# x added to the last stage's root rows on GpSimd, shares of two experts from five operations, first scatters without a bound

## The chip, the cores and the metric

The kernel runs on one core of a Trainium2 chip. The metric is the device time of one execution in microseconds; the times shown are medians of several executions. The engines that matter are TensorE (PE: matrix products and transposes), VectorE (DVE), ScalarE (ACT), GpSimd (POOL: here powers of small columns, and the starting of scatters by row index) and SyncE (SP, which starts most transfers). Times within the trace are microseconds from the start of the span.

## The reference, cut to what matters

```python
# x: 3125 x 256, 50000 edges (src, dst)
h   = relu(sage(layernorm(x), W1_l, W1_r, b1))
x   = x + sage(h, W2_l, W2_r, b2)          # sage: mean over neighbours @ W_l + own row @ W_r + b
t   = layernorm(x)
p   = softmax(t @ router_w.T);  rw, re = top_k(p, 2)
rw  = rw / max(rw.sum(-1), 1e-12)          # the shares of the two experts chosen
out = x + t + sum over e of combine[:, e] * (gelu(t @ w1[e] + b1[e]) @ w2[e] + b2[e])
```

## The kernel before

The 3125 nodes are 25 tiles of 128 rows (the last has 53). A dense adjacency matrix of 25 x 25 blocks stays in SBUF in 16 bits, so the mean over neighbours is 25 products of 128x512 a tile. The program has four stages: projection of the normalised x, aggregation of the first layer with projection for the second, aggregation of the second layer together with routing (the "last stage" of the graph part, tile by tile, from about 291 to 446 us), and rounds of the experts (from 470 us to the end). The change lies in the third of these; I call it stage 3.

In stage 3 each tile t goes through this loop. PE adds up 25 products (L1306) into one of four PSUM buffers; among the products of tile t+2 stands the transposition of the normalised rows of tile t (`turn_token`, L1380, ahead of the fourth product), then its router scores (L1391), and once in four tiles three small products of `prefix` (L1398 to L1401, ahead of the eighth product). SP loads two buffers for each tile: `zi`, the root rows (own row @ W2_r + b2) from DRAM, and `xt`, the rows of x. There is one of each, so SP waits for the semaphore `zx_taken` before it loads the next tile (`node_tile`, L456 and L457). On the same queue SP also stores the finished row sums of the tile, and in tiles 8 to 15 it starts three loads of expert weights a tile, after the store and ahead of the next tile's loads.

DVE's part of a tile is `x2_and_var` (L1008: zi + xt; L1012 and L1013: plus both halves of PE's sum, scaled; L1016 to L1019: mean and variance), then, after GpSimd's power (`root`, L581), `norm_and_sum` (L1026: normalised rows, which PE transposes; L1031: the row sum that SP stores). After tiles 4, 8, 12, 16, 20 and 23, and once more at the end, DVE runs `choose` for a batch of up to four tiles: it finds the two best experts, makes 0/1 masks for PE's `prefix` (up to L1063) and the two shares (L1066 to L1072). In tiles 6, 10, 14, 18, 22 and 24, and at the end, `place` turns PE's prefix sums into row numbers (`slots`, L1095). GpSimd, which executes in program order, starts two scatters a tile (L593; tile 0: L589, with a bound on the row numbers) as soon as the slots of the batch are there; a scatter of tile t-6 is queued behind the power of tile t. Ahead of the first power stand eight plain transfers (L605). At the end of the stage, scatters of tiles 17, 18 and 19 stand between the powers of tiles 23 and 24, and those of tiles 20 to 24 behind them.

DVE and GpSimd operate on `rows` (which holds xt and zi), `zt` (the row sum), `stat` and columns of `onehots`.

## Time and profile before

| | us |
|---|---|
| median of 3 runs | 595.81 |
| lowest, highest | 594.27, 596.04 |
| the profiled execution | 592.88 |
| its span | 591.2 |
| PE busy | 554.3 |
| DVE busy | 364.7 |
| GpSimd busy | 185.5 |
| mean granted clock of PE | 0.984 |

PE is busy in nearly all of the span. The exceptions are the first slice of 15 us and the passage from stage 3 to the experts, at 444 to 470 us. A row of the trace gives start, duration, engine, line, operation, tile written and tiles read, and in square brackets the idle time just before and what ended it.

### The profile page before, as it was taken

The numbers are of one execution on the slowest core, as the hardware profiler recorded it, in microseconds if no ns is written. First come the engines' busy times: TensorE is split into PE (matmuls) and PEld (weight loads), VectorE is DVE, ScalarE is ACT, GpSimd is POOL, SyncE is SP. The second block draws the span as 40 slices with busy tenths as digits, with TensorE's granted clock in tenths as the row PEclk, the third lists the DMA queues.
The fourth block names the chain that finished last, engine by engine and source line by source line (L and its number), as shares of the span: only waits on it lengthen the run. The fifth ranks groups of instructions, "written<-read, shape, count | busy, mean of one in ns | idle before, by whom it ended". The sixth has DMA issues, their size and how long they took to land.

```text
span 591.2 us, 11509 instructions
## 1 busy us (share of the span) xinstructions
PE 554.3 (94%) x3050; PEld 336.3 (57%) x3051; DVE 364.7 (62%) x1219; ACT 222.2 (38%) x422; POOL 185.5 (31%) x180
## 2 busy tenths in 40 slices
PE   4999999999999999999999999999991499999996
PEld 3555555555555555555445555555551488888885
DVE  5998667667657667663255766767678334444442
ACT  4676845434444434443101100000000155555554
POOL 3751000000000000000040154443356237787887
PEclk9999999999999999999999999999996799999999
DMA  8421211111111111012642146673332757787776
GB/s 259 148 79 60 65 45 54 48 34 54 44 37 55 37 44 54 28 55 53 196 129 80 55 137 200 202 245 126 106 130 97 228 109 118 125 142 129 129 116 92
DMA packets 64343, 61.24 MB, mean 104 GB/s; under 512 B 11281, under 2 KB 62334, under 8 KB 64302
## 3 DMA queue, kind: packets, MB, share of 16 engines
q1 hardware_dynamic: 47422, 44.84, 25.2%
q0 software_dynamic: 11200, 14.40, 13.1%
q10 hardware_dynamic: 5680, 1.49, 1.2%
q8 instruction: 21, 0.34, 0.2%
q14 instruction: 20, 0.16, 0.1%
HBM read 32.34 MB, written 29.30 MB: 104 GB/s over the span
## 4 chain that ended last, share of the span: by engine, by line
PE 69%; DMA 9%; DVE 8%; issue 8%; POOL 4%; SPq 1%; ACT 0%; POOLq 0%; DVEq 0%; ACTq 0%
PE bank L1306 22%; PE counts_ps L1448 8%; PE bank L1459 8%; PE bank L1221 8%; PE bank L1296 7%; PE counts_ps L662 7%; PE counts_ps L1306 4%; POOL xs_dram L593 2%; DMA rows<-in_x 2%; PE counts_ps L1439 2%; DMA xs_dram<-w,onehots 2%; DMA y<-y_dram 2%; PE bank L1211 1%; POOL stat L581 1%; PE bank L1289 1%
## 5 line engine op out<-in xcount | busy, mean ns | idle before, releaser
L1306 PE MATMUL bank<-y,adj 128*128 128x512 f16 x625 | 154.7, 379 | 0.4 <-ACT zt L1519 0.4
L1306 PE MATMUL counts_ps<-y,adj 128*128 128x512 f16 x625 | 144.0, 379 | 2.0 <-DMA y<-y_dram 2.0
L669 ACT ACTIVATE adj<-counts_ps 128x1000 f32 (+1 forms) x80 | 80.2, 1005 | 59.2 <-PE counts_ps L662 59.2
L635 POOL DMA_INDIRECT out<-adj x56 | 88.4, 1578 | 37.9 <-ACT adj L1654 18.5
L1306 PEld LDWEIGHTS counts_ps<-y,adj 128*128 128x128 f16 x625 | 60.7, 101 | 64.7 <-DMA y<-y_dram 4.3
L1306 PEld LDWEIGHTS bank<-y,adj 128*128 128x128 f16 x625 | 57.9, 97 | 59.5 <-issue 13.7
L565 POOL IOTA onehots<- 128x8 int32 x1 | 0.1, 143 | 225.4 <-PE counts_ps L662 225.4
L1448 PE MATMUL counts_ps<-adj 128*128 128x256 f32 x240 | 57.0, 380 | 0.0
L662 PEld LDWEIGHTS counts_ps<-onehots 125*128 125x128 f16 x640 | 42.4, 98 | 23.6 <-ACT adj L669 11.0
L648 DVE TENSOR_TENSOR onehots<-iota,lo_t 125x1024 f16<-125x1024 f16 x80 | 54.7, 684 | 1.8 <-issue 0.9
L1618 ACT ACTIVATE rows<-bank 128x256 f32<-128x256 f32 x25 | 9.6, 384 | 123.0 <-PE bank L1380 123.0
L648 DVE TENSOR_TENSOR onehots<-iota,key_t 125x1000 f16<-125x1000 f16 x80 | 53.7, 671 | 0.0
L1459 PE MATMUL bank<-adj 128*128 x224 | 53.0, 379 | 0.0
L662 PE MATMUL counts_ps<-onehots 125*128 125x125 f16 x640 | 51.0, 221 | 0.3 <-DVE onehots L648 0.3
L1221 PE MATMUL bank<-w,rows 128*128 128x512 f32 x100 | 48.8, 611 | 1.5 <-issue 1.3
L1448 PEld LDWEIGHTS counts_ps<-adj 128*128 128x128 f32 x240 | 44.9, 190 | 7.2 <-issue 1.2
L1296 PE MATMUL bank<-w,rows 128*128 128x512 f32 x100 | 47.0, 592 | 0.0
L1459 PEld LDWEIGHTS bank<-adj 128*128 128x128 f32 x224 | 40.5, 190 | 4.4
L1654 ACT ACTIVATE adj<-adj 128x256 f32<-128x256 f32 x56 | 25.4, 501 | 46.0 <-DVE adj L1175 46.0
L581 POOL TENSOR_TENSOR stat<-stat 128x1 f32<-128x1 f32 x25 | 14.2, 570 | 72.8 <-DVE stat L1019 72.8
L1175 DVE TENSOR_TENSOR adj<-bank,adj 128x512 f32<-128x512 f32 x28 | 19.4, 691 | 27.1 <-PE bank L1459 27.1
L1512 ACT ACTIVATE yo<-bank,scl_i 128x256 f16<-128x256 f32 x23 | 10.9, 475 | 58.1 <-PE bank L1296 58.1
(237 smaller groups left out, 646.6 us busy)
## 6 DMA issues: line engine op xcount, KB each, us to landing
adj<-xs_dram SPq DMA_DIRECT2D x31, 264.0 KB
rows<-z_dram SPq DMA_DIRECT2D x49, 128.0 KB, 2.1
z_dram<-zt SPq DMA_DIRECT2D x33, 128.0 KB, 1.7
adj<-in_L_ffn_w SPq DMA_DIRECT2D x16, 256.0 KB, 3.2
rows<-in_x SPq DMA_DIRECT2D x24, 128.0 KB
out<-yo SPq DMA_DIRECT2D x24, 128.0 KB
y_dram<-yo SPq DMA_DIRECT2D x23, 128.0 KB, 1.7
y<-y_dram SPq DMA_DIRECT2D x4, 640.0 KB, 6.8
```

The source lines that it names most:

```text
L581: g.tensor_tensor(stat[:, 8:9], stat[:, 9:10], stat[:, 10:11], ALU.pow).then_inc(S["rstd_in"], 1)
L635: g.indirect_dma_start(out, bass.IndirectOffsetOnAxis(ap=ids[u][:, h:h + 1], axis=0), ye[u][:, h, :], None, bounds_check=N - 1, oob_is_err ...
L648: last = nc.vector.tensor_tensor(oh[0:RUN, slot, :].rearrange("p (g k w) -> p g k w", k=n, w=HALF), iota_4[0:RUN, 0:n, :].rearrange("p (g ...
L662: last = nc.tensor.matmul(counts_ps[:, 2 * slot + bank_of, at * P:at * P + KEYS], stat_g[:, :, h:h + 1].rearrange("p k a -> p (k a)"), mov ...
L669: nc.scalar.activation(adj[:, :, bass.ds(at, GW * WD)].rearrange("p b (h d) -> p b h d", d=WD), counts_ps[:, 2 * (group % 2):2 * (group % ...
L1175: v.tensor_tensor(ysum[s], y_ps[s], ew(eb2_sb, e, 0).rearrange("p (h n) -> p h n", h=1) .to_broadcast((P, 2, D)), ALU.add).then_inc(S["ysu ...
L1221: last = te.matmul(out_of[t % 2][:, :], nrm_t_of[t % 2][:, k * P:(k + 1) * P], w[:, k, :], start=(k == 0), stop=(k == KD - 1))
L1296: last = te.matmul(bank[1][:, :], nrm_t[:, k * P:(k + 1) * P], w[:, k, :], start=(k == 0), stop=(k == KD - 1))
L1306: last = te.matmul(to, adj[:, b, t * P:(t + 1) * P], y[:, b, :], start=(b == 0), stop=(b == NT - 1))
L1448: last = te.matmul(hid_ps[s][:, m * PAIR:(m + 1) * PAIR], w1_of[s][:, k, m * P:(m + 1) * P], xe_t[s][:, k * PAIR:(k + 1) * PAIR], start=(k ...
L1459: last = te.matmul(y_ps[s][:, h, :], ge_t[s][:, m * PAIR + h * P:m * PAIR + (h + 1) * P], ew(ew2_sb, e, m), start=(m == 0), stop=(m == KD ...
L1654: a.activation(ye[u][:, h, :], ysum[s][:, h, :], ACT.Copy, scale=tab_c[:, bass.ds(i * 2 + h, 1)]).then_inc(S["ye_in"], 1)
```

## The change

Three things. First, the addition zi + xt leaves DVE (L1008 is gone). GpSimd does it in place into `xt` (`add_root`) and signals `x_added`. DVE's first operation of a tile now reads PE's sum and `xt`, and only this operation frees both buffers for the next loads. Second, the shares come from five operations in place of seven: both exponentials are summed on their own, this sum is bounded below by 1e-12 times the sum of all eight, and the exponentials are multiplied by its reciprocal. Third, the two scatters of tile 0 no longer have a bound.

```diff
+            def add_root(t):
+                pool.wait_ge(S["z_in"], 16 * (t + 1 + NT))
+                pool.wait_ge(S["x_in"], 16 * (t + 1))
+                g.tensor_tensor(xt[:, :], xt[:, :], zi[:, :], ALU.add).then_inc(S["x_added"], 1)
+
             def scatter(t, j):
...
                 for k in range(TOPK):
-                    if t == 0:
-                        g.indirect_dma_start(xs_dram, bass.IndirectOffsetOnAxis(
-                            ap=slots[:, t * TOPK + k:t * TOPK + k + 1], axis=0), tok[t % KEPT], None,
-                            bounds_check=NE * REGION - 1, oob_is_err=False).then_inc(scattered[t % 2], 16)
-                    else:
...
             pool.sem_inc(S["tok_free"], KEPT)
+            add_root(0)
...
                 root(t)
+                if t + 1 < NT:
+                    add_root(t + 1)
                 if BATCH + 2 <= t < NT - 1:
                     scatter(*to_scatter[t - BATCH - 2])
...
-                dve.wait_ge(S["z_in"], 16 * (t + 1 + NT))
-                dve.wait_ge(S["x_in"], 16 * (t + 1))
-
+                dve.wait_ge(S["x_added"], t + 1)
...
-                v.tensor_tensor(zt[:, :], zi[:, :], xt[:, :], ALU.add).then_inc(S["zx_taken"], 1)
-                dve.wait_ge(S["zx_taken"], t + 1)
                 dve.wait_ge(S["agg"], t + 1 + NT)
                 d = rdeg[:, bass.ds(t, 1)]
-                link(v.scalar_tensor_tensor(zt[:, :], counts_ps[:, s, 0:D], d, zt[:, :], ALU.mult, ALU.add))
+                v.scalar_tensor_tensor(zt[:, :], counts_ps[:, s, 0:D], d, xt[:, :], ALU.mult, ALU.add
+                                       ).then_inc(S["zx_taken"], 1)
+                dve.wait_ge(S["zx_taken"], t + 1)
...
+                v.tensor_reduce(resum, ex[:, :, 0:TOPK], AX.X, ALU.add)
                 link(v.tensor_reduce(esum, ex, AX.X, ALU.add))
+                link(v.scalar_tensor_tensor(esum, esum, 1e-12, resum, ALU.mult, ALU.max))
                 link(v.reciprocal(resum, esum))
-                link(v.tensor_tensor(prob, ex[:, :, 0:TOPK], each(resum, TOPK), ALU.mult))
-                link(v.tensor_reduce(esum, prob, AX.X, ALU.add))
-                link(v.tensor_scalar(esum, esum, 1e-12, None, ALU.max))
-                link(v.reciprocal(resum, esum))
```

GpSimd's queue at the start of stage 3, before: the eight plain transfers, then seven powers (tiles 0 to 6) and the scatters of tile 0.

```order
L605 DMA xs_dram<-biases 32x264 [waits zeros]
L605 DMA xs_dram<-biases 32x264 x7
L581 TENSOR_TENSOR stat<-stat 128x1 [waits var_in] x7
L589 DMA xs_dram<-w,onehots 27648x264 [waits slots]
L589 DMA xs_dram<-w,onehots 27648x264
```

The same place now (the power is L580, the addition L585).

```order
L604 DMA xs_dram<-biases 32x264 [waits zeros]
L604 DMA xs_dram<-biases 32x264 x7
L585 TENSOR_TENSOR rows<-rows 128x256 [waits x_in,z_in]
L580 TENSOR_TENSOR stat<-stat 128x1 [waits var_in]
L585 TENSOR_TENSOR rows<-rows 128x256 [waits x_in,z_in]
```

The addition of tile 0 now stands behind the eight transfers, and each later one behind the power of the tile ahead of it, where it waits for two loads.

GpSimd's queue at the end of stage 3, before, from the scatters of tile 17 to the power of tile 24.

```order
L593 DMA xs_dram<-w,onehots 27648x264 [waits slots]
L593 DMA xs_dram<-w,onehots 27648x264
L593 DMA xs_dram<-w,onehots 27648x264 [waits scattered0,slots]
L593 DMA xs_dram<-w,onehots 27648x264
L593 DMA xs_dram<-lo_t,onehots 27648x264 [waits slots]
L593 DMA xs_dram<-lo_t,onehots 27648x264
L581 TENSOR_TENSOR stat<-stat 128x1 [waits var_in]
```

The same place now.

```order
L585 TENSOR_TENSOR rows<-rows 128x256 [waits x_in,z_in]
L592 DMA xs_dram<-w,onehots 27648x264 [waits slots]
L592 DMA xs_dram<-w,onehots 27648x264
L592 DMA xs_dram<-w,onehots 27648x264 [waits scattered0,slots]
L592 DMA xs_dram<-w,onehots 27648x264
L592 DMA xs_dram<-lo_t,onehots 27648x264 [waits slots]
L592 DMA xs_dram<-lo_t,onehots 27648x264
L580 TENSOR_TENSOR stat<-stat 128x1 [waits var_in]
```

The addition of tile 24 stands ahead of six scatters, and the power of tile 24 still behind them.

DVE's queue of one tile, before, and behind it the same piece now.

```order
L1008 TENSOR_TENSOR zt<-rows 128x256 [waits u_ready,x_in,z_in]
L1012 SCALAR_TENSOR_TENSOR zt<-counts_ps,rdeg,zt 128x256 [waits agg,zx_taken]
L1013 SCALAR_TENSOR_TENSOR zt<-counts_ps,rdeg,zt 128x256 [waits dve_chain]
L1016 BN_STATS stat<-zt 128x6 [waits sums_free]
L1018 BN_AGGR stat<-stat 128x2 [waits dve_chain]
L1019 TENSOR_SCALAR stat<-stat 128x1 [waits dve_chain]
```

```order
L1010 SCALAR_TENSOR_TENSOR zt<-counts_ps,rdeg,rows 128x256 [waits agg,u_ready,x_added]
L1013 SCALAR_TENSOR_TENSOR zt<-counts_ps,rdeg,zt 128x256 [waits zx_taken]
L1016 BN_STATS stat<-zt 128x6 [waits sums_free]
L1018 BN_AGGR stat<-stat 128x2 [waits dve_chain]
L1019 TENSOR_SCALAR stat<-stat 128x1 [waits dve_chain]
```

The operation that frees the load buffers now also waits for PE's sum of the tile (`agg`).

## Rows read from the trace of the kernel before

**Rows 1.** The page, busy time of each engine with its share.

```profile
PE 554.3 (94%) x3050; PEld 336.3 (57%) x3051; DVE 364.7 (62%) x1219; ACT 222.2 (38%) x422; POOL 185.5 (31%) x180
```

**Rows 2.** Busy time by stretch: stretch, length, PE, PEld, DVE, ACT, POOL, clock, DMA.

```profile
355.00:380.00 25.00, 25.00 (x139) 13.43 (x136) 17.22 (x75) 1.77 (x5) 10.44 (x12) 1.00 0.70 219
```

**Rows 3.** Timeline, start of stage 3: start, duration, engine, operation, count, [idle before].

```profile
300.07 4.16 POOL L605 DMA_DIRECT2D xs_dram<-biases  x8 [0.49 <-DVE biases L986]
...
304.25 0.61 POOL L581 TENSOR_TENSOR stat<-stat 128x1 f32<-128x1 f32 x1
304.97 0.41 DVE L1026 TENSOR_SCALAR w<-zt,stat 128x256 f32<-128x256 f32 x1 [1.73 <-POOL stat L581]
...
305.91 0.38 PE L1380 MATMUL bank<-ident,w 128*128 128x128 f32 x2
...
311.88 0.38 PE L1380 MATMUL bank<-ident,w 128*128 128x128 f32 x2
```

**Rows 4.** Groups by form, engine POOL: busy us, mean ns of one, idle before.

```profile
L527 POOL IOTA iota<- 128x256 f16 x1 | 1.5, 1517 | 0.0
...
L530 POOL TENSOR_SCALAR_AFFINE_SELECT ident<-ident 128x128 f32<-128x128 f32 x1 | 0.3, 283 | 0.0
...
L567 POOL TENSOR_SCALAR_AFFINE_SELECT onehots<-onehots 128x1 f32<-128x1 f32 x1 | 0.2, 187 | 26.4 <-DVE onehots L983 26.4
```

**Rows 5.** Timeline of tiles 5 and 6, where DVE is catching up.

```profile
331.55 0.42 DVE L1008 TENSOR_TENSOR zt<-rows 128x256 f32<-128x256 f32 x1
332.01 0.48 DVE L1012 SCALAR_TENSOR_TENSOR zt<-counts_ps,rdeg,zt 128x256 f32<-128x256 f32 x1
332.16 0.33 SPq L456 DMA_DIRECT2D rows<-z_dram  x1
...
334.09 0.55 POOL L581 TENSOR_TENSOR stat<-stat 128x1 f32<-128x1 f32 x1 [8.01 <-DVE stat L1019]
...
335.99 0.42 DVE L1008 TENSOR_TENSOR zt<-rows 128x256 f32<-128x256 f32 x1 [0.37 <-DMA rows<-in_x]
```

**Rows 6.** Timeline, DVE's L1008 of tiles 9, 12, 13 and 17.

```profile
355.28 0.42 DVE L1008 TENSOR_TENSOR zt<-rows 128x256 f32<-128x256 f32 x1
...
371.37 0.42 DVE L1008 TENSOR_TENSOR zt<-rows 128x256 f32<-128x256 f32 x1 [1.32 <-DMA rows<-in_x]
...
379.67 0.42 DVE L1008 TENSOR_TENSOR zt<-rows 128x256 f32<-128x256 f32 x1
...
403.37 0.42 DVE L1008 TENSOR_TENSOR zt<-rows 128x256 f32<-128x256 f32 x1
```

**Rows 7.** Timeline: the masks of the batch of tiles 8 to 11 and PE's prefix.

```profile
378.25 0.16 DVE L1063 TENSOR_TENSOR onehots<-onehots 128x16 f16<-128x16 f16 x1
...
378.83 0.18 PE L1398 MATMUL bank<-onehots 128*128 128x32 f16 x1
```

**Rows 8.** Timeline: shares and slots of the last batch.

```profile
454.76 0.18 DVE L1066 TENSOR_REDUCE onehots<-onehots 128x4 f32<-128x32 f32 x1
...
456.08 0.17 DVE L1072 TENSOR_TENSOR key_t<-onehots 128x8 f32<-128x8 f32 x1
...
457.63 0.17 DVE L1095 CAST onehots<-onehots 128x8 uint32<-128x8 f32 x1
```

**Rows 9.** Timeline of POOL from the power of tile 23 to the last scatter.

```profile
439.43 0.57 POOL L581 TENSOR_TENSOR stat<-stat 128x1 f32<-128x1 f32 x1 [0.97 <-DVE stat L1019]
...
443.95 0.96 POOL L593 DMA_INDIRECT xs_dram<-w,onehots  x1 [1.46 <-DMA xs_dram<-w,onehots]
...
448.73 0.61 POOL L581 TENSOR_TENSOR stat<-stat 128x1 f32<-128x1 f32 x1
...
456.17 0.96 POOL L593 DMA_INDIRECT xs_dram<-onehots  x1 [0.30 <-issue]
458.62 0.96 POOL L593 DMA_INDIRECT xs_dram<-onehots  x1 [1.50 <-DVE onehots L1095]
...
462.42 0.96 POOL L593 DMA_INDIRECT xs_dram<-w,onehots  x1 [0.31 <-issue]
```

More of the change, by code:

```diff
@@ L233, in build @@
         resum = later([BATCH], F32)
-        prob = later([BATCH, TOPK], F32)
         hist = later([NB + 1, NE], F32)
@@ L587, in scatter @@
                 for k in range(TOPK):
-                    if t == 0:
-                        g.indirect_dma_start(xs_dram, bass.IndirectOffsetOnAxis(
-                            ap=slots[:, t * TOPK + k:t * TOPK + k + 1], axis=0), tok[t % KEPT], None,
-                            bounds_check=NE * REGION - 1, oob_is_err=False).then_inc(scattered[t % 2], 16)
-                    else:
-                        g.indirect_dma_start(xs_dram, bass.IndirectOffsetOnAxis(
-                            ap=slots[:, t * TOPK + k:t * TOPK + k + 1], axis=0),
-                            tok[t % KEPT], None).then_inc(scattered[t % 2], 16)
+                    g.indirect_dma_start(xs_dram, bass.IndirectOffsetOnAxis(
+                        ap=slots[:, t * TOPK + k:t * TOPK + k + 1], axis=0),
+                        tok[t % KEPT], None).then_inc(scattered[t % 2], 16)
                 if 0 < t <= NT - KEPT:
```

5 lines of the change are left out of this document (3 added, 2 removed).

## Prediction

> **What bounds the kernel.** I read the page's busy times first, then busy time by stretch for stage 3, then the timeline at its start, in its laps and at its end. PE is busy for 94% of the span [rows 1], and inside stage 3 for 25.00 of 25 us at full clock, while DVE has 17.22 and GpSimd 10.44 of them [rows 2]. So within the stage DVE and GpSimd cost nothing as long as PE is never kept waiting, and every moment in which it is goes straight into the time. PE's beat is 311.88 - 305.91 = 5.97 us a tile [rows 3], and four tiles with one prefix take about 23.97 us (4 x 5.97 and some 0.07 for the prefix). Behind the stage, from 444 to 470 us, PE idles and a serial chain decides: power of tile 24, its normalised rows, scores, masks, slots, the last four scatters, their landing, the first loads of the experts. What GpSimd and DVE lose or gain there counts in full, too.
>
> **The new operation's price.** The trace has no addition of 128x256 on GpSimd. A select over one input of 128x128 took 283 ns and of 128x1 187 ns [rows 4]: 0.75 ns a column, so 256 columns from one input would be 0.38 us, and two inputs read one after the other 0.57 us. DVE needs 0.42 for the same addition [rows 5]. Upward the nearest row is an iota of 128x256 with 1.52 us [rows 4]. I take 0.7 us, near the doubled select; bounds 0.4 and 1.5.
>
> The Trainium skill (GPSIMD Engine Reference, section 3, Performance versus the Vector engine) has a two-input addition of 2048 fp32 columns at 4497 ns on GpSimd against 2293 ns on DVE, and its rule is to leave elementwise work to VectorE; scaled to 256 columns its slope alone would be an estimated 0.56 us, and the sum below would stay within 0.3 us of mine. No run here shows it yet.
>
> **Start of the stage: +2.4.** This term is the surest. GpSimd is busy with eight plain transfers until 304.23, and the power of tile 0 starts at 304.25 [rows 3]. The addition of tile 0 now stands behind the same transfers, where DVE before could add without GpSimd. Addition 304.25 to 304.95, 0.1 for the signal, DVE's first operation at 305.05. From this operation to the power it takes 334.09 - 332.01 = 2.08 us [rows 5], from the power to the normalising operation 304.97 - 304.25 = 0.72 [rows 3], so that one runs from 307.85 to 308.26. PE transposed that tile at 305.91, 0.53 after the rows were ready [rows 3]; now it can at 308.3. PE waits 2.4 us (2.1 with an addition of 0.4, 3.2 with 1.5). It has no other work ahead of this in its queue, and as it is then busy without a gap to the end of the stage, nothing gives this back.
>
> **The laps: +0.5.** Before, DVE's addition freed the buffers before PE's sum had to be there. Now the first operation that also needs PE's sum frees them, and the addition follows the landing. A lap in which DVE catches up is thus: operation 0.48, SP starts 0.19 after it (332.16 against 331.97), from SP's start to the landing 3.83 (335.99 - 332.16) [rows 5], addition 0.7, signal 0.1: 5.3 us, where it was 4.44 (335.99 - 331.55). It still beats PE's 5.97, so in most laps this is hidden behind PE's products. In the laps with choose DVE gets 0.46 shorter by the addition and about 0.55 by the shares (below), which pays back more than one such lap.
>
> The tight place is tiles 8 to 15, where three loads of weights stand ahead of the next tile's loads on SP's queue. Tile 9 to 13 took 379.67 - 355.28 = 24.39 us, tile 13 to 17 23.70 [rows 6], against 23.97 of PE; DVE stood waiting for the load, 1.32 us ahead of tile 12. After the change: the lap with choose -1.01; three laps bound by a transfer +0.86 each (0.7 + 0.1 + 0.06, since 0.48 stands where 0.42 did) = +2.58; in two of them SP's loads are held by the store of an earlier tile, which DVE delivers 0.46 earlier, -0.92. Sum +0.65: 25.04 and 24.35. DVE falls behind PE by 1.07, then by 0.38 more. On GpSimd's queue the power of the next tile also comes some 0.2 late: addition and two scatters (1.27 each, the spacing of the last four in rows 9) end 2.5 to 2.8 after DVE's first operation of the tile, and the power is due 2.08 after it. What PE can bear: the masks were ready at 378.41, PE's prefix ran at 378.83 [rows 7], a margin of 0.42, and DVE had then fallen behind by 0.44 already, so 0.86 in all. 1.07 + 0.2 exceeds this by 0.4; the next batch adds little, because PE's wait has itself reset the distance. I put 0.5 us of waiting of PE here, with 0 to 3 as ends.
>
> **The end of the stage: +0.6.** The power of tile 23 started at 439.43 [rows 9], so DVE's first operation on PE's sum began 2.08 ahead, at 437.35. Its loads are freed 0.48 later, start after 0.19, land after 3.83: 441.85. The addition of tile 24 ends at 442.55, then come six scatters, the first at 442.75 and 1.27 apart, the last ending near 450.1. Before, the same six included 1.46 us of waiting for a landing [rows 9], which the later start swallows. So the power of tile 24 starts near 450.2 instead of 448.73: +1.45, and the whole chain behind it with it. Back come the shares of the last batch: L1066 to L1072 were 456.08 - 454.76 = 1.32 us for six steps of 0.22 [rows 8]; four steps remain, the first of which has no wait behind it, so 0.44 to 0.6, say 0.55. The slots come at 457.80 + 1.45 - 0.55 = 458.7, and GpSimd is free of the scatters ahead at 457.13 + 1.45 = 458.6. Before, the first of the last four started 0.82 after the slots; now it starts between 0.3 behind the one ahead and 0.8 behind the slots: 458.9 to 459.5 instead of 458.62. I take +0.6. The experts' rounds behind it are not touched.
>
> **Nothing:** the bound of the first two scatters. They lie at tiles 6 and 7, GpSimd idles there, and PE has its beat. If GpSimd were full there, it would be a few tenths at most, as two starts of this kind are 2.4 us in all.
>
> **Sum:** 2.4 + 0.5 + 0.6 = 3.5 us. On the profiled execution 592.88 + 3.5 = 596.4. The median of the runs is 595.81, 2.93 above that execution; taken from there 599.3, +0.58%.
>
> **Rivals.** (a) *The lap becomes the beat.* If the addition takes 0.9 or more, or a load lands 0.2 later than in rows 5, the laps at the weights grow by another 0.6 a batch, and the other batches (three laps of 5.5 and one of about 7.3) stop making up ground. PE then waits for the masks in tiles 4, 12 and 16 and for the rows of tile 23: some 3 us instead of 0.5. Then 595.81 + 2.6 + 3 + 0.6 = 602.0; with 1.5 us for the addition, about 2.5 us a batch over five batches, near 612. For it: DVE stood waiting for loads already. Against: the doubled select is under 0.6.
>
> (b) *Same.* The addition costs 0.4, the laps nothing, and at the end the late queue is made good by the landing wait and the shares: 2.1 + 0 - 0.6 = 1.5, time 597.3. For it: 1.46 of waiting at the end was there to be used. Against: the scatters there begin 2.55 us later (442.75 against 440.2).
>
> (c) *Faster.* DVE sets the stage: it waits for loads in tiles 6 and 12 [rows 5, 6], and it loses the addition in 25 laps (0.46 each) and 0.55 in each choose. It could only be if PE were not full; as it is [rows 2], this mechanism acts at the end alone, where shares and addition give 1.0. It decides only if PE reads the rows of tile 0 late enough not to wait, which needs GpSimd free some 2.4 us earlier than 304.23. Then 595.81 - 1.0 = 594.8.
>
> **How the numbers follow.** My forecast (start 2.0 to 2.7, laps under 1.5, end 0 to 1.2) 0.6; (a) 0.2; (b) 0.15; (c) 0.05. About 0.3%, 1.8 us, is what a measurement of this kernel can tell from no change. The forecast's own range is 597.8 to 601.2 (2.0 + 0 + 0 to 2.7 + 1.5 + 1.2), above 595.81 + 1.8 = 597.6, so it and (a) are slower, (b) with 597.3 is same, (c) faster; rounded for the edges, slower 0.78, same 0.16, faster 0.06. The range for 8 in 10 takes in most of (a) and of (b): 596.8 to 604.5.
>
> **What would show it.** Right: in the new profile PE has a wait of about 2.4 us behind the normalised rows of its first transposition of stage 3; the addition on GpSimd is 0.6 to 0.8 us; DVE's longest waits move from loads to GpSimd's addition; the power of tile 24 starts some 1.4 us later against PE's last product; the shares span about 0.8 in place of 1.32. Wrong: no wait of PE at the start (then the transfers ahead of the addition don't hold it); PE waits at every prefix (then the lap is the beat, rival a); the last scatter starts earlier against PE's last product than before (then the end gives time back).

## The result and the profile after

The changed kernel is slower, and by more than forecast. Three series were measured, each beside the kernel before:

| series | changed, median (lowest to highest) | before | ratio, 95% interval |
|---|---|---|---|
| first | 604.06 (600.92 to 605.71) | 595.19 | 1.0163 [1.0131, 1.0195] |
| second (`after_again`) | 602.10 (601.15 to 604.09) | 594.46 | 1.0133 [1.0101, 1.0165] |
| third (`after_third`) | 602.29 (600.89 to 602.72) | 594.03 | 1.0142 [1.0125, 1.0159] |

That is +8.9, +7.6 and +8.3 us where +3.5 was forecast. The profiled execution of the first series took 600.92 us, its span is 599.2: +8.0 against the 591.2 of before. In the changed kernel the power is L580, the addition L585, the scatters L592; DVE's first operation of a tile is L1010; PE's products are L1305, its transposition L1379, its prefix L1397.

Page of the changed kernel, busy time of each engine with its share (before: [rows 1]).

```profile
PE 557.5 (93%) x3050; PEld 338.4 (56%) x3051; DVE 352.5 (59%) x1180; ACT 222.1 (37%) x422; POOL 204.6 (34%) x205
```

DVE lost 12.2 us of work and GpSimd got 19.1 us, while PE has 3.2 us more in a span that is 8.0 longer. So 4.8 of the 8.0 us is idle time of PE. Four key times of the two profiles divide it:

| stretch | before | after | difference |
|---|---|---|---|
| up to PE's transposition of tile 0 | 305.91 | 308.34 | +2.43 |
| from there to that of tile 23 (the laps) | 135.20 | 136.99 | +1.79 |
| from there to the start of the last scatter | 21.31 | 23.16 | +1.85 |
| from there to the experts' first rows | 7.84 | 8.13 | +0.29 |
| from there to the end | 120.94 | 122.58 | +1.64 |

The first row also holds the stages ahead, which the change doesn't touch: PE's first product of stage 3 starts at 291.23 before and at 291.33 after, and between 290.3 and 293.2 us over all profiles. From this product to the transposition of tile 0 it is 14.68 us before and 17.01 after, so the start itself costs 2.33.

**The start.** Timeline of the changed kernel, to be held against [rows 3]: start, duration, engine, operation, [idle before and what ended it].

```profile
300.15 4.15 POOL L604 DMA_DIRECT2D xs_dram<-biases  x8 [0.49 <-DVE biases L988]
...
304.32 0.74 POOL L585 TENSOR_TENSOR rows<-rows 128x256 f32<-128x256 f32 x1
305.09 0.48 DVE L1010 SCALAR_TENSOR_TENSOR zt<-counts_ps,rdeg,rows 128x256 f32<-128x256 f32 x1 [4.47 <-POOL rows L585]
...
307.87 0.41 DVE L1026 TENSOR_SCALAR w<-zt,stat 128x256 f32<-128x256 f32 x1 [0.79 <-POOL stat L580]
...
308.34 0.44 PE L1379 MATMUL bank<-ident,w 128*128 128x128 f32 x2 [2.22 <-DVE w L1026]
```

The addition stands directly behind the eight plain transfers, DVE has waited 4.47 us for it, and PE waits 2.22 us for the rows. The forecast had 305.05, 307.85 and 308.3 for the last three rows.

**The laps.** DVE's first operation of tiles 9 to 13 and, after the dots, 17.

```profile
357.38 0.48 DVE L1010 SCALAR_TENSOR_TENSOR zt<-counts_ps,rdeg,rows 128x256 f32<-128x256 f32 x1
363.12 0.48 DVE L1010 SCALAR_TENSOR_TENSOR zt<-counts_ps,rdeg,rows 128x256 f32<-128x256 f32 x1 [2.11 <-POOL rows L585]
368.59 0.48 DVE L1010 SCALAR_TENSOR_TENSOR zt<-counts_ps,rdeg,rows 128x256 f32<-128x256 f32 x1 [1.42 <-POOL rows L585]
375.08 0.48 DVE L1010 SCALAR_TENSOR_TENSOR zt<-counts_ps,rdeg,rows 128x256 f32<-128x256 f32 x1 [2.47 <-POOL rows L585]
382.77 0.48 DVE L1010 SCALAR_TENSOR_TENSOR zt<-counts_ps,rdeg,rows 128x256 f32<-128x256 f32 x1
...
407.68 0.48 DVE L1010 SCALAR_TENSOR_TENSOR zt<-counts_ps,rdeg,rows 128x256 f32<-128x256 f32 x1
```

Tile 9 to 13 takes 25.39 us and tile 13 to 17 24.91, against 24.39 and 23.70 in [rows 6] and 23.97 of PE. In three of the four laps DVE stands waiting for GpSimd's addition. The lap of tile 12 in SP's and GpSimd's rows:

```profile
369.13 0.35 SPq L472 DMA_DIRECT2D adj<-in_L_ffn_b  x1
370.02 0.35 SPq L455 DMA_DIRECT2D rows<-z_dram  x1
...
374.32 0.72 POOL L585 TENSOR_TENSOR rows<-rows 128x256 f32<-128x256 f32 x1 [2.69 <-DMA rows<-in_x]
```

The buffer was free at 368.59 + 0.48 = 369.07, but SP was starting the third load of weights then. The load started at 370.02 and the addition 4.30 later. With 0.76 from addition to DVE this lap is 375.08 - 368.59 = 6.49 us, longer than PE's 5.97. DVE's lateness then reaches PE, first through the masks; the three rows are the prefixes of tiles 8 to 11, 12 to 15 and 20 to 22.

```profile
382.11 0.19 PE L1397 MATMUL bank<-onehots 128*128 128x32 f16 x1 [0.63 <-DVE onehots L1063]
...
407.02 0.19 PE L1397 MATMUL bank<-onehots 128*128 128x32 f16 x1 [0.76 <-DVE onehots L1063]
...
448.80 0.19 PE L1397 MATMUL bank<-onehots 128*128 128x32 f16 x1 [0.78 <-DVE onehots L1063]
```

Before, the first two had no wait and the last 0.29 us. In the profiles of the second and third series the first two waits were 0.15 and 1.15, and 0.52 and 0.49.

**The end of the stage.** GpSimd's queue from the power of tile 23 to the last scatter, to be held against [rows 9].

```profile
444.03 0.57 POOL L580 TENSOR_TENSOR stat<-stat 128x1 f32<-128x1 f32 x1 [0.74 <-DVE stat L1019]
447.20 0.72 POOL L585 TENSOR_TENSOR rows<-rows 128x256 f32<-128x256 f32 x1 [2.60 <-DMA rows<-in_x]
448.09 1.03 POOL L592 DMA_INDIRECT xs_dram<-w,onehots  x1 [0.17 <-issue]
...
454.49 0.96 POOL L592 DMA_INDIRECT xs_dram<-lo_t,onehots  x1 [0.30 <-issue]
455.46 0.59 POOL L580 TENSOR_TENSOR stat<-stat 128x1 f32<-128x1 f32 x1
...
464.70 0.95 POOL L592 DMA_INDIRECT xs_dram<-onehots  x1 [1.11 <-DVE onehots L1094]
...
468.49 0.96 POOL L592 DMA_INDIRECT xs_dram<-w,onehots  x1 [0.30 <-issue]
```

GpSimd idles 2.60 us for the load of tile 24 with six scatters queued behind the addition, and the power of tile 24 comes behind all of them. SP had started that load at 442.11:

```profile
442.11 0.34 SPq L476 DMA_DIRECT2D rows<-z_dram  x1
```

So it took 5.09 us to the addition, not the 3.83 of the forecast. The shares of the last full batch, against [rows 8]:

```profile
448.66 0.15 DVE L1066 TENSOR_REDUCE onehots<-onehots 128x4 f32<-128x8 f32 x1
...
449.35 0.17 DVE L1070 TENSOR_TENSOR key_t<-onehots 128x8 f32<-128x8 f32 x1
```

0.69 us in place of 1.32, in this batch as in the last. The addition over all tiles, in the groups by form (busy us, mean ns of one, idle before):

```profile
L585 POOL TENSOR_TENSOR rows<-rows 128x256 f32<-128x256 f32 x25 | 19.3, 773 | 33.3 <-DMA rows<-in_x 33.3
```

**What the addition does to DVE.** One of the steps towards the masks of the last full batch, before:

```profile
442.84 0.19 DVE L1057 TENSOR_TENSOR onehots<-onehots 128x32 f16<-128x32 f32 x1
```

The same step now, beside the addition of tile 24 (447.20 to 447.92), and behind it the addition of tile 23 with DVE's L1031, which takes 0.42 to 0.43 us alone:

```profile
447.37 0.60 DVE L1057 TENSOR_TENSOR onehots<-onehots 128x32 f16<-128x32 f32 x1
```

```profile
439.89 0.72 POOL L585 TENSOR_TENSOR rows<-rows 128x256 f32<-128x256 f32 x1 [0.49 <-DMA rows<-in_x]
439.97 0.92 DVE L1031 TENSOR_TENSOR yo<-zt,onehots 128x256 f32<-128x256 f32 x1
```

The step of 0.19 us ended 0.05 behind the addition, L1031 0.28 behind it. Other steps were held in the same way: L1052 0.49 instead of 0.17 in the batch of tiles 12 to 15, and in the second profile L1047 of that batch 0.65 instead of 0.19, where PE then waited 1.15. Not every DVE operation beside an addition is longer: L1040 and L1050 kept their times. So the moved addition takes time from DVE now and then, just ahead of the masks that PE waits for. The forecast has no such term.

**PE's clock.** Busy time by stretch for PE: stretch, length, PE with its instructions, granted clock, DMA share, GB/s. First the profile of the first series, then that of `after_again`.

```profile
309.00:312.00 3.00, 3.00 (x18) 1.00 0.40 125
```

```profile
306.00:309.00 3.00, 1.43 (x7) 0.94 0.33 90
309.00:312.00 3.00, 3.00 (x10) 0.50 0.43 131
```

Both had the same wait of 2.2 us just before. In one the clock stayed at its upper level of 2.4 GHz, in the other it fell to 1.2 GHz for about 3.3 us (1-us stretches 308 to 313: 0.82, 0.50, 0.50, 0.50, 0.98), in which half the work is done: some 1.7 us lost. This is in no term of the forecast.

### The profile page after: what moved, and what is told of

It reads as the page before. It is cut to its first block, busy times and chain, and to the rows that moved or that the text cites. A ratio compares the mean times of both kernels' runs of the same rounds, so it can differ in the third digit from the quotient of the medians.

```text
span 599.2 us, 11493 instructions
## 1 busy us (share of the span) xinstructions
PE 557.5 (93%) x3050; PEld 338.4 (56%) x3051; DVE 352.5 (59%) x1180; ACT 222.1 (37%) x422; POOL 204.6 (34%) x205
## 4 chain that ended last, share of the span: by engine, by line
PE 83%; DMA 5%; issue 4%; POOL 3%; DVE 3%; SPq 1%; ACT 0%; POOLq 0%; DVEq 0%; ACTq 0%
PE bank L1305 22%; PE counts_ps L1305 16%; PE counts_ps L1447 9%; PE bank L1458 8%; PE bank L1220 8%; PE bank L1295 7%; PE counts_ps L664 7%; PE counts_ps L1438 2%; DMA rows<-in_x 2%; PE bank L1390 1%; POOL xs_dram L592 1%; PE bank L1210 1%; DMA y<-y_dram 1%; PE bank L1288 1%; DMA xs_dram<-w,onehots 1%
## 5 line engine op out<-in xcount | busy, mean ns | idle before, releaser
L1305 PE MATMUL bank<-y,adj 128*128 128x512 f16 x625 | 154.7, 379 | 0.4 <-ACT zt L1518 0.4
L1305 PE MATMUL counts_ps<-y,adj 128*128 128x512 f16 x625 | 144.2, 379 | 1.9 <-DMA y<-y_dram 1.9
L1305 PEld LDWEIGHTS counts_ps<-y,adj 128*128 128x128 f16 x625 | 60.7, 101 | 64.7 <-DMA y<-y_dram 4.2
L1305 PEld LDWEIGHTS bank<-y,adj 128*128 128x128 f16 x625 | 57.9, 97 | 59.5 <-issue 13.7
L1010 DVE SCALAR_TENSOR_TENSOR zt<-counts_ps,rdeg,rows 128x256 f32<-128x256 f32 x25 | 12.1, 484 | 34.0 <-POOL rows L585 21.4
```

What stands on the lines that cost most here:

```text
L1010: v.scalar_tensor_tensor(zt[:, :], counts_ps[:, s, 0:D], d, xt[:, :], ALU.mult, ALU.add).then_inc(S["zx_taken"], 1)
L1305: last = te.matmul(to, adj[:, b, t * P:(t + 1) * P], y[:, b, :], start=(b == 0), stop=(b == NT - 1))
```

## The experiments

The theory at the outset: three places delay PE on their own (start, laps, end), each because the addition now stands in GpSimd's queue or because the buffers are freed later; the shares only give back. Its rivals: the addition's own length decides; the late freeing alone decides; the extra time is PE's clock. Single profiles of all kernels, by the same key times (the end here goes from tile 23's transposition to the power of tile 24 alone):

| kernel | transposition of tile 0 | laps | end | first rows to end |
|---|---|---|---|---|
| before | 305.91 | 135.20 | 7.62 | 120.9 |
| after (three profiles) | 308.34, 307.57, 308.08 | 136.99, 138.64, 136.62 | 10.13, 10.74, 10.21 | 122.6, 122.6, 123.0 |
| e1 shares alone | 305.84 | 135.20 | 7.28 | 123.4 |
| e2 addition alone | 308.94 | 140.08 | 10.30 | 123.0 |
| e3 addition of tile 0 first | 307.19 | 139.08 | 10.88 | 124.0 |
| e4 sum in its own buffer | 308.58 | 136.10 | 8.50 | 123.9 |
| e5 last addition later | 310.25 | 139.17 | 7.49 | 121.2 |
| e6 after, 22 fillers | 308.62 | 137.10 | 10.41 | 121.0 |
| e8 = e3 + e4 + e5 | 307.31 | 135.26 | 7.48 | 122.9 |
| e11 addition twice | 308.61 | 144.18 | 11.54 | 124.2 |
| e12 before, late freeing | 306.19 | 135.63 | 6.49 | 122.5 |
| e7 before, 22 fillers | 305.03 | 136.01 | 6.84 | 120.8 |
| e13 e1, 22 fillers | 306.01 | 135.20 | 6.47 | 120.9 |
| e14 after, fillers at the start | 308.07 | 136.53 | 10.21 | 122.7 |
| e15 e14, 22 fillers | 308.41 | 136.69 | 10.16 | 122.9 |

Two things help to read it. From PE's first product of stage 3 to the transposition of tile 0 it is 14.6 to 14.9 us in before, e1, e7, e12 and e13, 17.0 in the changed kernel's three profiles, e2, e5, e6, e14 and e15, 15.25 in e3, 15.05 in e8, 17.5 in e4 and 17.7 in e11. And the end of before varies, too: 7.62 in its own profile, but 6.84 in e7 and 6.49 in e12, where GpSimd waits 0.68 and 0.30 ahead of the third scatter in place of 1.46.

### e1_shares: the five operations alone

```diff
+                v.tensor_reduce(resum, ex[:, :, 0:TOPK], AX.X, ALU.add)
                 link(v.tensor_reduce(esum, ex, AX.X, ALU.add))
+                link(v.scalar_tensor_tensor(esum, esum, 1e-12, resum, ALU.mult, ALU.max))
                 link(v.reciprocal(resum, esum))
-                link(v.tensor_tensor(prob, ex[:, :, 0:TOPK], each(resum, TOPK), ALU.mult))
...
```

> The kernel before with the five-operation shares alone. Theory T (the loss has three places: the start of stage 3 +2.4, the laps +1.8, the queue of scatters at its end +2.5, and PE's clock behind it +1.3): the shares are not among them, shares of the last batch take 0.8 us instead of 1.32, the last scatter starts 0.5 us earlier, time 0.5 below before (594.7 against 595.2), too little for the interval. Rival R (the shares cost through their new use of DVE): slower than before.

Measured: 593.86 against 594.54, ratio 0.9984 [0.9964, 1.0003]. DVE's timeline in the last batch:

```profile
454.25 0.15 DVE L1065 TENSOR_REDUCE onehots<-onehots 128x4 f32<-128x8 f32 x1
...
454.94 0.17 DVE L1069 TENSOR_TENSOR key_t<-onehots 128x8 f32<-128x8 f32 x1
```

0.69 us again, 0.63 less than in [rows 8]. The time is 0.7 lower, which the interval doesn't quite tell from nothing. The shares cost nothing that can be measured, and hardly help.

### e2_add_only: the addition alone

The changed kernel with the seven operations and the bound of the first scatters restored.

> The changed kernel with the seven-operation shares and the bound of the first scatters as before, so the moved addition alone. T: all of the loss is the addition's: 0.5 to 1.5 us above the changed kernel's 604.1, since in the laps with choose DVE gets no 0.55 us back (masks come before the shares, so only the next lap feels it). R: about 595.2.

Measured: 605.63, ratio 1.0173 [1.0129, 1.0217]. All of the loss is with the addition. PE waits 2.8 us in its laps behind the masks, at least twice as long as with the shorter shares (1.4, 1.3 and 1.0 in the three profiles); DVE has 0.6 us more to do in each `choose`. By these waits the shares are worth more beside the addition than they are alone; the medians don't tell e2 from the changed kernel (the intervals overlap).

### e3_add0_first: the first addition ahead of the plain transfers

```diff
+            add_root(0)
             pool.wait_ge(S["zeros"], 1)
...
             pool.sem_inc(S["tok_free"], KEPT)
-            add_root(0)
```

> The changed kernel with the addition of tile 0 ahead of the eight plain transfers. T: PE's wait of 2.2 us at its first transposition of stage 3 goes, the rest stays, PE's waits for masks in tiles 12 and 16 the same 0.6 to 0.8 us: 604.1 - 2.4 = 601.7. Rival L (the laps set the beat, and the start only took what they would have taken): the waits reappear in the laps and the time stays at 604.

Measured: 602.68 (600.30 to 604.30), ratio 1.0118 [1.0066, 1.0170]. PE's waits in its profile:

```profile
PE bank L1379 <- DVE w L1026: 0.4, 1, 0.4
PE bank L1397 <- DVE onehots L1063: 1.6, 1, 1.6
```

The wait at the start is 0.4 in place of 2.2 us, so the cause of that term is shown: the eight transfers ahead. Most of what is left is DVE's L1026, which takes 0.75 us instead of 0.41 beside the addition of tile 1 (306.24). The time did not follow clearly: the interval overlaps those of the changed kernel. In the profiled execution, one of its two long ones, a wait of 1.6 us comes at 406 us, and behind it the granted clock is 0.50 from 408 to 410. A reading that fits, from this one profile, is that without the late start DVE's lateness has less distance to PE; then the start and the laps are not independent terms.

### e4_own_buffer: the sum in a buffer of its own

```diff
-                sp.wait_ge(S["zx_taken"], t + 1)
+                sp.wait_ge(S["x_added"], t + 1)
...
-                g.tensor_tensor(xt[:, :], xt[:, :], zi[:, :], ALU.add).then_inc(S["x_added"], 1)
+                if t > 0:
+                    pool.wait_ge(S["zx_taken"], t)
+                g.tensor_tensor(nrm[:, :], xt[:, :], zi[:, :], ALU.add).then_inc(S["x_added"], 1)
```

DVE reads `nrm`, and the addition itself frees the load buffers.

> The changed kernel with the sum written to a buffer of its own (the free nrm), and the loads of the next tile started when GpSimd has added, not when DVE has read. T: the loads no longer wait for PE's sum, DVE never waits for the addition after tile 2, PE has no wait for masks in tiles 12 and 16 (-1.8), the addition of tile 24 no longer waits for its load (some -1.9 on the power of tile 24); the start stays: 600 to 601. L (GpSimd's own time of 0.75 a tile is what counts, not where its load waits): no more than -0.5, 603.5.

Measured: 600.01, ratio 1.0090 [1.0061, 1.0119], as expected; the lowest ratio of the changed kernel's three is 1.0133 [1.0101, 1.0165]. The laps take 136.10 with one wait of 0.7 in them (136.99 and 136.62 in the profiles of the changed kernel whose clock stayed up, with 1.4 and 1.0), the end 8.50. The start is worse: PE waits 2.76 us there, since the addition of tile 1 now comes early enough to hold DVE's normalising operation.

```profile
307.65 0.88 DVE L1028 TENSOR_SCALAR w<-zt,stat 128x256 f32<-128x256 f32 x1 [0.79 <-POOL stat L580]
307.66 0.72 POOL L587 TENSOR_TENSOR rows<-rows 128x256 f32<-128x256 f32 x1
```

In [rows 3] this operation takes 0.41. The later freeing of the buffers is part of the loss both in the laps and at the end.

### e5_end_order: the last addition two scatters later

```diff
-                if t + 1 < NT:
+                if t + 1 < NT - 1:
                     add_root(t + 1)
...
                 if t == NT - 2:
+                    add_root(t + 1)
                     scatter(*to_scatter[t - BATCH - 1])
```

> The changed kernel with the addition of tile 24 behind the scatters of tile 17 and ahead of those of tile 18, where its load has landed. T: two scatters run in the 2.6 us in which GpSimd waited for that load, the power of tile 24 starts 7.6 us after PE's transposition of tile 23 instead of 10.1, the last scatter 2 us earlier or less where the slots become late instead; time 1.5 to 2.5 below the changed kernel. Rival: the landing of the load is what everything waits for, and nothing moves.

Measured: 602.73, ratio 1.0143 [1.0121, 1.0164], no lower than `after_again` beside it. GpSimd's timeline has what was expected:

```profile
451.21 0.73 POOL L585 TENSOR_TENSOR rows<-rows 128x256 f32<-128x256 f32 x1
...
456.91 0.60 POOL L580 TENSOR_TENSOR stat<-stat 128x1 f32<-128x1 f32 x1
```

The addition has no wait ahead of it any more, and the end is 7.49 in place of 10.1 to 10.7. That the median did not follow is a miss. The profiled execution has the gain: from PE's first product of stage 3 to the experts' first rows it took 184.9 us, 2.9 less than the 187.8 of `after_again`, in which the clock fell at the same place. But its stage 3 began at 293.23, 1.9 to 2.7 us later than in the changed kernel's profiles, ahead of all that the edit touches. The three other executions were no shorter, and they have no trace. So why the 2.6 to 3.2 us of the end are not in the median stays open; in e8 the same edit stands in a time that is 6 us lower.

### e6_fillers, e7_before_fillers, e13_shares_fillers: PE's clock at the experts

The kernel runs 14 products of no use ahead of the experts' first rows (L1467). These three have 22.

```diff
-    FILLERS = 14
+    FILLERS = 22
```

> The changed kernel with 22 fillers (products that only keep PE at work ahead of the experts' rounds) in place of 14. C (PE's clock falls back to half at the start of the rounds in most executions, 0.52 to 0.63 granted from 477 to 481 us, because PE stood idle between its fillers and the first rows): the clock stays at 1.00 there, 1.6 us less from the first rows to the end, which is 121 us. Rival: the fillers have nothing to do with it, 122.6 to 124 us as in the other profiles, or the first rows come later by the fillers' length.

> The kernel before with 22 fillers in place of 14 and nothing else. C: 593 to 593.5 against 594.5, and 120.9 us from the first rows to the end. Rival: within 0.3 us of before, because the first profile of before (120.9 us) is its usual run.

> The kernel before with the five-operation shares and 22 fillers in place of 14. C: PE's clock stays at full from the first rows of the experts on, as with 22 fillers in the changed kernel (1.6 us less from the first rows to the end than in most runs), and the shares give 0.5: 592.4 to 593 against 594.5, faster than both kernels. Rival: before keeps the clock anyway in its runs, as in its first profile, and only 0.5 remains: 594.

Measured: e6 601.20, 1.0116 [1.0094, 1.0138], against 1.0133 for the changed kernel beside it; e7 593.40, 0.9993 [0.9976, 1.0009]; e13 592.54, 0.9989 [0.9970, 1.0007]. PE from 476 to 482 us, in the changed kernel of the first series and in e6:

```profile
476.00:482.00 6.00, 4.59 (x19) 0.72 0.51 137
```

```profile
476.00:482.00 6.00, 4.56 (x31) 1.00 0.54 137
```

The same busy time holds 19 instructions at 0.72 and 31 at 1.00. The way from the first rows to the end was 120.8 to 121.0 us in the profiles of e6, e7 and e13, where the clock stayed up, and 122.5 to 124.2 in most profiles with 14 fillers. The profiles of before, with 120.9, and of e5, with 121.2, were the exceptions. So the +1.64 in the table of the result is this: an execution of before without the fall of the clock was set against the usual one. The medians give no sign that it is part of the loss: with 22 fillers in both kernels the ratios are 1.0116 and 0.9993, 1.2% apart, close to the 1.3 to 1.6% with 14. The times of e7 and e13 lie where they were expected, but the kernel before beside them was at 593.85, and against it the gain is 0.45 and 1.31 us, which the intervals don't tell from nothing. So both expectations of a gain missed. e15, below, has 122.9 with 22 fillers, so these don't keep the clock up in every execution.

### e8_repaired: the three repairs together

e3, e4 and e5 in one kernel.

> The changed kernel with all three repairs: tile 0's addition ahead of the transfers, the sum in a buffer of its own, tile 24's addition behind the scatters of tile 17. T: if the losses add, 604 - 1.2 (start, as measured) - 3 (laps and load of the last tile) - 1.5 (end) = 598 to 599, still above before by the start's remaining 1.3 and the laps' remaining 0.9. Rival (GpSimd's additions cost in themselves, 19 us of busy time): above 600.

Measured: 596.20 (594.78 to 596.86), ratio 1.0030 [1.0015, 1.0044]: 5.9 us under `after_again`, and 2 us better than expected. PE's transpositions and prefixes that waited:

```profile
307.31 0.44 PE L1382 MATMUL bank<-ident,w 128*128 128x128 f32 x2 [0.23 <-DVE w L1029]
```

```profile
446.56 0.19 PE L1400 MATMUL bank<-onehots 128*128 128x32 f16 x1 [1.31 <-DVE onehots L1066]
```

There is no wait in the laps, 135.26 as before the change, and the granted clock is 1.00 from 306 to 441 us. Whether the three give more together than alone isn't settled: against `after_again`, by the ratios, they give 0.9, 2.6 and -0.6 us alone, 2.9 in sum, and 6.1 together; against the first series 8.2 in sum and 7.9 together. What remains against before are the places where the addition stands beside DVE. At the start L1029 takes 0.75 us (306.50) instead of 0.41, and PE waits 0.23. At the end a conversion of DVE, 0.25 us in the same place before the change, ends only with the addition of tile 24, and PE waits 1.31 for the masks behind it, against 0.29 before:

```profile
444.06 1.05 DVE L1055 CAST onehots<-onehots 128x8 f32<-128x8 uint32 x1
```

```profile
444.35 0.73 POOL L587 TENSOR_TENSOR rows<-rows 128x256 f32<-128x256 f32 x1
```

### e11_double_add: the addition twice

```diff
+                g.tensor_tensor(nrm[:, :], xt[:, :], zi[:, :], ALU.add)
                 g.tensor_tensor(xt[:, :], xt[:, :], zi[:, :], ALU.add).then_inc(S["x_added"], 1)
```

> The changed kernel with GpSimd's addition executed twice (once more into a free buffer ahead of the real one), so each addition stage costs some 0.75 us more. T (the laps stand at the edge; each tenth on a lap that is bound by its load is PE's waiting once DVE has fallen 0.9 us behind): PE waits 3.0 at the start instead of 2.2, and in the laps 6 to 9 us instead of 1.8 to 3.9; time 609 to 613. Rival (GpSimd's addition is hidden in the laps; the loss there comes from where the loads are freed): start +0.75, end +0.75, laps as before, about 604.

Measured: 611.72, ratio 1.0305 [1.0273, 1.0338], as expected. In PE's waits from 312 to 465 us (us in total, times, longest):

```profile
PE bank L1398 <- DVE onehots L1064: 5.1, 4, 2.4
```

The second addition takes 0.74 us on average and adds 9.6 us to the median of `after_again`, thirteen times its length: by the profiles 0.6 of waiting at the start, 5.5 to 7.6 in the laps, 0.8 to 1.4 at the end. PE now waits behind four batches of masks, not three, and 0.80 for the rows of tile 23: 4.6 us of waiting up to that tile, against 1.0 to 1.4. Part of the rest is clock: besides the fall behind the start there is a second one behind the wait of 2.4 us, with 0.50 at 388 and 389 us. If the laps had room, the second addition would cost nothing in them. That they sit on the edge of PE's beat, as rival (a) has it, is shown by this run.

### e12_late_free: the late freeing alone, on DVE

```diff
-                v.tensor_tensor(zt[:, :], zi[:, :], xt[:, :], ALU.add).then_inc(S["zx_taken"], 1)
-                dve.wait_ge(S["zx_taken"], t + 1)
+                link(v.tensor_tensor(xt[:, :], zi[:, :], xt[:, :], ALU.add))
...
+                v.scalar_tensor_tensor(zt[:, :], counts_ps[:, s, 0:D], d, xt[:, :], ALU.mult, ALU.add
+                                       ).then_inc(S["zx_taken"], 1)
```

The kernel before, whose load buffers are freed behind the operation on PE's sum.

> The kernel before, in which DVE still adds zi to x, but in place into xt, so that the load buffers are freed by the operation after it, which also needs PE's sum: the changed kernel's way of freeing without GpSimd. T: a lap bound by its load grows by about 0.5 instead of 1.3, no loss at the start (DVE adds at once) and none at the end's queue; PE waits 0.5 to 2 us behind masks of tiles 12 and 16; time 595 to 596.5 against 594.5. Rival (late freeing is the whole loss of the laps): 1.8 to 3.9 us in the laps, 597 to 598.

Measured: 593.92 against 593.85, ratio 0.9997 [0.9976, 1.0018]; the laps took 135.63. One prefix waited in them:

```profile
403.50 0.19 PE L1399 MATMUL bank<-onehots 128*128 128x32 f16 x1 [0.25 <-DVE onehots L1064]
```

Freed late, but with DVE's addition of 0.42 directly behind the landing and no queue of GpSimd, the laps still hold. The late freeing by itself costs nothing that can be measured. Together with e4: it uses up the margin, and the longer way over GpSimd then goes beyond it.

### e14_start_fillers, e15_both_fillers, after_third: PE kept busy in its wait

```diff
+                pe.wait_ge(S["nrm_t_in"], t + 2 * NT)
+                if t == 0:
+                    for k in range(10):
+                        te.matmul(bank[0][:, k % KD * P:(k % KD + 1) * P], ident[:, :], ident[:, :], start=True, stop=True)
                 pe.wait_ge(S["normed"], t + 1 + NT)
-                pe.wait_ge(S["nrm_t_in"], t + 2 * NT)
```

> The changed kernel with ten products of the identity with itself (128 x 128) on TensorE while it waits for the first normalised rows of stage 3; they go into the buffer that the transposition behind them overwrites. Theory G (the idle time behind the late start drops TensorE's granted clock to 0.50 in some executions: in the profiles of four kernels with this wait the clock was 0.50 for some 3.3 us from about 309 us, in three others it stayed at 1.00): the clock is 1.00 from 306 to 316 us, and the executions in which it would have fallen are 1.6 us shorter, so the median comes about 0.8 to 1.6 us under that of the changed kernel beside it, its lowest time is unchanged, and its highest comes down. Rival (the fall is made good by slack behind it, or costs nothing): clock the same, median within 0.4 us of the changed kernel. Second rival: the ten products run beyond the wait and delay the first transposition: it starts later than 308.6 us, and the time rises.

> The same with 22 fillers in place of 14 ahead of the experts' first rows as well. Theory G: both causes of a low clock are gone, so the executions scatter less than those of the changed kernel; median 600 to 601 us, about 1 us under the kernel with the 22 fillers alone had against the kernel before (ratio 1.0116), that is 1.009 to 1.011, with a granted clock above 0.975 in every execution. Rival: ratio 1.0116 or above.

> The changed kernel itself beside the two, for comparison. From its two earlier series: median 602 to 604 us. Theory G: its executions scatter by some 3 us, the longer ones have the lower mean granted clock (0.971 against 0.975 before), and the profiled one shows either 1.00 throughout from 306 to 316 us and a lap time of stage 3 near 137.0 us, or 0.50 for some 3.3 us and a lap time near 138.6. Rival: no relation between clock and time.

Measured: e14 602.57, 1.0149 [1.0129, 1.0169]; e15 600.94, 1.0114 [1.0097, 1.0131]; the changed kernel 602.29, 1.0142 [1.0125, 1.0159]. PE's timeline in e14:

```profile
305.73 2.39 PE L1379 MATMUL bank<-ident 128*128 128x128 f32 x20
308.07 0.44 PE L1382 MATMUL bank<-ident,w 128*128 128x128 f32 x2
```

The products fill the wait and end with it, the transposition is not delayed, and the clock is 1.00 from 306 to 360 us. But the median did not fall: by the median the rival was right. One thing stands against reading it so: in the profiles of e14 and e15 the experts' first rows come 9.57 and 9.51 us after the start of the last scatter, in all others 7.8 to 8.7. These 1 to 1.4 us belong to neither theory, and they can hide a gain of that size; where they come from is not known. e15 is 1.3 us lower than the kernel beside it, inside its expectation in time but not by its ratio (1.009 to 1.011 expected); its interval overlaps the other's, its executions scatter no less, and e6 had nearly the same ratio without the fillers at the start. `after_third` showed a clock of 1.00 at the start and laps of 136.62, one of the two cases it was to show.

Over the three series of the changed kernel there are 12 executions. The five with a mean granted clock of 0.975 or more took 600.89 to 602.19 us, median 601.15; the seven with 0.974 or less took 602.38 to 605.71, median 603.74. The fall behind the start is seen in the profiles of `after_again`, e2, e5 and e11 (about three us at 0.50, and laps longer by about 1.7 than the waits explain) and not in those of after, `after_third`, e4 and e6. So a low mean clock goes with the long executions of the same kernel; how much of the +8 of the median it makes, and at which place, isn't settled.

## Why the prediction was right or wrong

**Direction and mechanism: right.** PE is full, and the loss came at the three places named. The size was wrong: the forecast's own range of 597.8 to 601.2 doesn't hold the medians of 602.1 to 604.1, and the change is more than twice the +3.5. That the time lies in the wide range, 596.8 to 604.5, is due to rival (a), for which that range was drawn. Two steps of the sum failed, the laps and the end; the wait of 3.83 us for a load, taken for both, is the term they share.

**Price of the addition, 0.7: nearly.** Alone it takes 0.72, on average 0.773, and up to 1.00 over the three profiles where DVE runs beside it, as at 308.35 (0.97) beside L1031, which reads two inputs. The Trainium skill (GPSIMD Engine Reference, Specifications) says that GpSimd shares its SBUF interfaces with VectorE and contends with DVE instructions with two SBUF inputs; these rows agree, with up to 0.28 us for one addition. The 0.56 us by the slope of its section 3 was too low, and so was the doubled select with 0.57; the 0.7 was a choice above both, and a good one. What the price left out is DVE's side: up to 0.8 us on an operation that is held by the addition.

**Start, +2.4: right, to 0.1 us.** Measured +2.33 from PE's first product of stage 3, wait of PE 2.22. e3, which moves the addition ahead of the transfers, takes the wait down to 0.4.

**Laps, +0.5: the first step that failed.** They took +1.8, +3.4 and +1.4 in the three profiles. Four terms of that step were too small or missing. (1) The load: the lap was costed with 3.83 from SP's start to the addition; in tiles 10 to 17 it was 3.72 to 4.32. Uncontended, in tiles 1 to 5, it was 2.6 to 2.7, so the 3.83 taken for normal was a middle value. At the weights it is mostly longer, 4.05 on average over tiles 10 to 17. Tile 9 to 13 was forecast at 25.04 and took 25.39, tile 13 to 17 24.35 and took 24.91. (2) The power was to come 0.2 late behind addition and scatters; it came 2.08 + 0.38 behind DVE's first operation in tiles 10 to 12 and 14 to 16. Both together: 0.35 + 0.18 more of lateness in the first batch, where 0.4 beyond the margin had been allowed, and then again in the next, which the forecast took to be nearly free because the wait "has itself reset the distance". (3) The clock: a wait of PE costs its length and, in some executions, some 1.7 us of half clock on top. This term is missing altogether. (4) DVE's steps that are held by the addition, such as 0.49 instead of 0.17 ahead of the masks at tile 16. This is missing, too.

**Rival (a) came nearest.** Its condition was an addition of 0.9 or a load 0.2 later than in rows 5; loads at the weights were up to 0.5 later. PE waited for the masks at tiles 12 and 16, as it said, not at tile 4 nor for the rows of tile 23, but for the masks of the last full batch. Its 3 us of waiting in the laps were 1.0 to 1.4, with clock and end making up the rest, so that its 602.0 is close to the medians of 602.1 to 604.1 is in part luck; its distance of 6.2 us is short of the measured 7.6 to 8.9. It had a chance of 0.2 and should have had more: that DVE already waited for loads at the weights [rows 6] stood in the text as the point for it, and the doubled select, the point against it, speaks of the addition only and not of the load.

**End, +0.6: the second step that failed.** The last scatter came 1.85 later against PE's transposition of tile 23 in the first profile, 2.40 in the second; against e7 and e12, in which before's queue waited less for a landing, it is 2.7 to 3.4. Mis-sized is the landing of tile 24: 5.09 and, in `after_again`, 5.6 us instead of 3.83. The forecast let the late queue of scatters start at 442.75, that is 5.4 behind DVE's first operation of tile 23 (437.35); measured it is 448.09 - 441.60 = 6.49, 1.1 more, and the power of tile 24 is later by the same. The 1.46 of waiting for a landing which the prediction let the later start swallow was indeed gone: the six scatters run 1.27 apart without a gap. The shares gave 0.63, forecast 0.55.

**Bound of the first scatters, 0:** no run has it alone; e2, which has it back, shows no gain of it.

**Experts' rounds, 0:** nothing in the medians speaks against it. The profile of before had them 1.6 us shorter than usual, which is part of the 2.93 us by which that execution lay under its median; starting the forecast from the median took care of it.

**The sum.** From PE's first product of stage 3 to the experts' first rows it is 179.0 us before, 185.3 and 185.2 in the two profiles of the changed kernel whose clock stayed up behind the start, and 187.8 in the one in which it fell: +6.2 and +8.8, against medians of +7.6 to +8.9. So the medians lie between the two, nearer the one with the fall of the clock; how often it fell in the executions without a trace is not known.

**Same and faster, rivals (b) and (c): wrong.** The addition was not 0.4. e8, with all three repairs, comes near (b) with 1.0030, but by another way than (b) had it. No version came out measurably faster than the kernel before; e13 is the lowest with 592.54, 0.9989 [0.9970, 1.0007].

## What to carry to other kernels

Before an operation is moved off an engine that isn't the bound, write down the loop that it closes (buffer free, load starts, load lands, operation, buffer free) and compare it with the bound's beat, with the load's length from the tiles with the most other traffic; where the trace already shows an engine waiting for that load, there is no margin. An operation that waits, set into the queue of an engine that also starts transfers, delays all that stand behind it, and order and a buffer of its own gave 5.9 of 7.6 us back here. Look at the other engine's rows beside the moved operation, too: here DVE steps of 0.2 us lasted until the addition was done. And compare like stretches, not whole spans: here the stages ahead vary by 3 us between executions.

## What the runs showed of the hardware

Some DVE operations beside GpSimd's addition of 128x256 ended only with it or up to 0.3 us behind it: 0.60 instead of 0.19 (after, 447.37), 1.05 instead of 0.25 (e8, 444.06), 0.88 instead of 0.41 (e4, 307.65), 0.92 instead of 0.42 (after, 439.97). Where L1031 had started first, the addition was the longer one, 0.97 instead of 0.72 (after, 308.35). L1040 and L1050 kept their times beside it.

A wait of TensorE of 1.6 to 2.8 us in full work was followed by some 3 us at half clock in some executions (1.65 in e3, 2.23 in `after_again`, 2.42 and 2.77 in e11), and not in others: after has the same wait as `after_again`, e4 one of 2.76. It makes the cost of a wait uncertain by some 1.7 us.

The loads of tiles 6, 18 and 22 took 3.6 to 4.3 us from SP's start to the addition, while their neighbours without weights took 2.6 to 3.0; tiles 10 and 14, at the weights, took 4.32 and 3.72. In the stretches of these five tiles the DMA rows show a packet of another queue. Queues of the changed kernel from 333.5 to 339 us (packets, MB, share):

```profile
q1 hardware_dynamic: 432, 0.39, 23.8%
q8 instruction: 1, 0.02, 1.5%
```

In the stretches of tiles 7, 9, 19 and 23, which have no such packet, the addition of the tile came 2.8 to 3.0 us after SP's start; in tile 6 it was 4.29. In tile 24 (5.09) a packet of a second instruction queue stands beside the load, with two scatters. It looks as if the fetching of code can delay a load that is under way. It doesn't always: in the profiles of `after_again` and `after_third` the load of tile 6 took 2.71 and 2.60 us, with such a packet in its stretch, too. The load of [rows 5], from which the forecast has its 3.83 us, is one that had a packet beside it (before, 332 to 336.2 us). All this was only read from traces; no run tested it.
